# A decoder layer on one core: one projection behind each of the first score bursts, three buffers for split terms, and some work given to other engines

## The chip, the cores and the metric

The kernel runs on one core of a Trainium2 chip. The metric is the device time of one execution in microseconds (us). The time before is the median of three runs. Readers of the profile meet five engines: PE (TensorE), DVE (VectorE), ACT (ScalarE), POOL (GpSimd) and SP (SyncE, which here only issues DMAs). Each goes through its own list of instructions in order and waits on semaphores.

## What is computed

One post-norm decoder layer on 32 sequences of 128 tokens with 128 features, 16 heads of width 8, all in float32 at the interface:

```
x = layernorm(x + self_attention(x))                  # softmax over 128 keys, q/k/v with biases
x = layernorm(x + cross_attention(ctx, x, ctx))       # one 8x8 matrix per q, k, v for all heads, then Wo
x = layernorm(x + ffn(x))
# ffn: out = qlinear(gelu(qlinear(x, W1, b1)), W2, b2)
# qlinear(x, W, b): x quantised with ONE min and max over the whole tensor (affine, 8 bit),
#                   W symmetric (8 bit), integer product, times both scales, plus b
```

The minimum and maximum over the whole tensor part the program in stages: nothing of the feed-forward can start before all of attention is done, and its second product waits for all of the gelu.

## The kernel before, in words

**Tasks and slots.** A task is one batch's attention of one kind, self ("S") or cross ("C"); 64 tasks stand in the list `SEQ`, always in pairs of batches. Six self pairs come first (`LEAD_PAIRS`), then cross and self pairs in turn, then the last cross pairs. The engines are written as loops over slots k from -5 to 67 (`over_slots`). In slot k PE computes the first scores of task k+2 and the second, shifted scores of tasks k and k-1, the products with v of task k-1, transposes for k-2 and the output projection for k-3; DVE takes the maxima of task k+2 (`maximum(0)` and `maximum(1)`, L944, each over eight heads), the reciprocal and scaling of k-2, the sum of k-3, and the normalisation (`new_x`, L936) five slots behind; ACT takes the exponentials (L759, L768) and the copies out of PSUM; POOL computes 1/sqrt of the variance (L584, L587) and splits. Slot -2 holds the first maxima.

**Bursts.** `scores(0)` and `scores(1)` on PE are the two bursts of a slot. Each writes half of the heads to PSUM (`ps_s1`, banks 0 and 1) for DVE's maximum and, interleaved, half of the shifted scores (`ps_s2`, banks 2 and 3) for ACT's exponential. A burst waits for the maximum and the exponential before, and the first burst of a pair waits until its stacks have landed (`stacks_landed`).

**Projections, splits and stacks.** q and k of a pair are projected for two batches at once (L1239, L1247), evacuated by ACT (L727) and split by POOL into a float16 high and low part (`split`, L403 and L405; pair 0 by DVE) in a tile of `parts`, of which each name (sq, sk, cq, ck) has two. SP then copies three terms of the parts to the rows of a "stack" in SBUF (`fill`, L438, three DMAs for each name); a stack is the operand of the score bursts, four stacks for each name. A split waits until the stacks of the pair two before have landed. For cross attention the queries' terms (cq) come from the transposed result of self attention. V is projected by L1253 and copied by ACT (L747). All three projections write bank 7 (`ps_p`), except k of pair 0.

**The ramp.** For slots below `LEAD_SLOTS` = 2 PE issues all projections of a slot behind the second burst, later at the end of the slot (`projections(k + 1)`), q and k of a pair together. POOL makes the masked weights (`blocks`) in slot -2, and PE's three setup products (`setup_products`) follow in slot 0. `xT_in` has two tiles (`LOADS`).

**The maximum rows.** The transposed maxima are scaled by ACT and go to the stacks by a small DMA of ACT's own (L771) in each slot.

**Tail and feed-forward.** In slots 62 to 67 DVE has no maxima left; it finishes the last tasks and takes extremes of the cross results (`x2_extremes`, L916 and L917). Then the extremes go over PE (`share_extremes`), DVE works out the scales, ACT and DVE quantise x, PE transposes it and multiplies with W1, ACT applies gelu (L813), DVE takes its extremes (L1060, L1061). Ahead of the second extremes PE computes ten products that nobody reads (`unread_products`, L1375).

## Time and profile before

| | us |
| --- | --- |
| median of three runs | 337.71 |
| lowest, highest | 335.9, 339.79 |
| profiled execution | 336.97 |
| its span, first to last instruction | 335.2 |
| busy: DVE, PE, ACT, POOL | 306.8, 268.9, 248.1, 196.8 |

The rows below come from one profiled execution; times are from the start of its span. In a timeline row stand the start, the length, the engine with its line, the operation, output and input; a bracket gives the idle time before it and what ended that. "SPq" and "ACTq" are issues of DMAs by SP and ACT. A row with "x2" is two instructions in a row. In a windows row stand the stretch, its length, then busy time and number of instructions for PE, PE's weight loads (PEld), DVE, ACT and POOL, then PE's granted clock as a share of full speed, the DMA engines' share and GB/s.

### The profile page before, as it was taken

To read this page: it belongs to the slowest core of one execution; us is meant where nothing else is said; L and a number is where in the kernel's file an instruction comes from. 1 tells how busy PE (TensorE), PEld (TensorE's weight loads), DVE (VectorE), ACT (ScalarE), POOL (GpSimd) and SP (SyncE) were. 2 spreads that over 40 slices of the span, in tenths; PEclk is the share of its full clock that TensorE was granted. 3 is DMA by queue.
4 is the path that set the end of the run, shared out by engine and by line. 5 is a ranking of instruction groups with operands and counts; after the bars stand their busy time and mean duration, and the time that the engine had idled before them with its cause. 6 is when DMAs were issued, how large, how long until landed. Compare 5 with 4: busy or idle time off the path is not lost.

```text
span 335.2 us, 12397 instructions
## 1 busy us (share of the span) xinstructions
PE 268.9 (80%) x4917; PEld 168.2 (50%) x4917; DVE 306.8 (92%) x705; ACT 248.1 (74%) x502; POOL 196.8 (59%) x397
## 2 busy tenths in 40 slices
PE   4678989799999999999999988798885267416981
PEld 3355656566666666566566655555553123102551
DVE  5668899899999999999999999889989779998995
ACT  2246889688988889888888887768773299910995
POOL 2856788887667676666666846855322113901395
PEclk9999999999999999999999999989998575757896
DMA  2452424244242342424423232321100000000026
GB/s 64 115 151 85 115 77 127 59 129 116 73 122 69 113 125 64 128 59 116 118 63 114 83 113 81 107 73 52 30 3 0 1 2 0 0 0 0 2 63 189
DMA packets 48992, 25.13 MB, mean 75 GB/s; under 512 B 6440, under 2 KB 48808, under 8 KB 48936
## 3 DMA queue, kind: packets, MB, share of 16 engines
q1 hardware_dynamic: 46504, 23.74, 24.5%
q8 instruction: 39, 0.64, 0.8%
q10 hardware_dynamic: 2432, 0.60, 0.8%
q14 instruction: 17, 0.14, 0.1%
HBM read 9.39 MB, written 2.10 MB: 34 GB/s over the span
## 4 chain that ended last, share of the span: by engine, by line
DVE 41%; POOL 24%; issue 19%; PE 6%; SPq 4%; DMA 3%; ACT 2%; POOLq 1%; DVEq 0%; ACTq 0%
DVE neg_max L944 15%; DVE h_ext L1060 5%; DVE h_ext L1061 5%; POOL rstd L587 5%; SPq L438 3%; DVE arena_q L1087 2%; POOL arena_h L615 2%; POOL var_eps L584 2%; DVE arena_q L936 2%; POOL parts_ck L405 2%; PE ps L1188 2%; POOL parts_cq L405 2%; DVE o_stats L1096 2%; POOL parts_cq L403 2%; POOL parts_ck L403 2%
## 5 line engine op out<-in xcount | busy, mean ns | idle before, releaser
L944 DVE TENSOR_REDUCE neg_max<-ps 128x8 f32<-128x1024 f32 x128 | 157.1, 1227 | 10.4 <-PE ps L1188 10.0
L768 ACT ACTIVATE probs<-ps 128x1024 f32<-128x1024 f32 x64 | 65.5, 1024 | 22.8 <-PE ps L1195 22.8
L759 ACT ACTIVATE probs<-ps 128x1024 f32<-128x1024 f32 x64 | 65.6, 1024 | 16.3 <-PE ps L1195 12.8
L1188 PE MATMUL ps<-arena_h 31*128 31x128 f16 x1024 | 52.4, 220 | 21.1 <-DVE neg_max L944 11.2
L1188 PEld LDWEIGHTS ps<-arena_h 31*128 31x128 f16 x1024 | 30.6, 94 | 55.6 <-DVE neg_max L944 38.3
L1195 PE MATMUL ps<-arena_h 32*128 32x128 f16 x1024 | 51.3, 217 | 0.6 <-ACT probs L768 0.6
L584 POOL TENSOR_TENSOR var_eps<-mean_var,eps_col 128x1 f32<-128x1 f32 x64 | 12.3, 192 | 65.8 <-DVE mean_var L928 65.8
L1216 PE MATMUL ps<-probs,arena_h 128*32 128x128 f32 x1024 | 42.3, 282 | 0.2 <-issue 0.2
L1216 PE MATMUL ps<-probs,arena_q 128*32 128x128 f32 x1024 | 41.2, 279 | 0.0
L587 POOL TENSOR_TENSOR rstd<-var_eps,minus_half 128x1 f32<-128x1 f32 x64 | 35.3, 551 | 5.2 <-POOL var_eps L584 0.3
L1195 PEld LDWEIGHTS ps<-arena_h 32*128 32x128 f16 x1024 | 29.3, 93 | 1.5 <-ACT probs L768 1.0
L1216 PEld LDWEIGHTS ps<-probs,arena_h 128*32 128x32 f32 x1024 | 24.6, 110 | 7.3 <-issue 0.6
L1216 PEld LDWEIGHTS ps<-probs,arena_q 128*32 128x32 f32 x1024 | 24.0, 109 | 6.7
L1305 PE MATMUL ps<-ident,u_sb 128*128 128x128 f32 x128 | 24.7, 275 | 0.0
L1320 PE MATMUL ps<-ident,att 128*128 128x128 f32 x64 | 21.2, 331 | 4.1 <-DVE att L963 4.1
L778 ACT COPY u_sb<-ps 128x256 f32<-128x256 f32 x64 | 23.4, 366 | 0.8 <-PE ps L1216 0.8
L1060 DVE TENSOR_REDUCE h_ext<-arena_h 128x1 f32<-128x1024 f32 (+1 forms) x17 | 19.5, 1147 | 2.8 <-ACT arena_h L813 2.8
L785 ACT COPY attT<-ps 128x128 f32<-128x128 f32 x64 | 18.0, 282 | 4.9 <-PE ps L1320 4.9
L1061 DVE TENSOR_REDUCE h_ext<-arena_h 128x1 f32<-128x1024 f32 (+1 forms) x17 | 19.5, 1146 | 0.0
L954 DVE RECIPROCAL r_sum<-ps 128x16 f32<-128x16 f32 x64 | 16.6, 259 | 2.5 <-PE ps L1305 2.5
L813 ACT ACTIVATE arena_h<-ps,b_sb,quant 128x1024 f32<-128x1024 f32 (+1 forms) x17 | 18.5, 1199 | 0.3 <-PE ps L1365 0.3
L1365 PE MATMUL ps<-xqT,w_q 128*128 128x512 bf16 x32 | 14.0, 577 | 5.2 <-ACT xqT L809 4.8
(168 smaller groups left out, 618.0 us busy)
## 6 DMA issues: line engine op xcount, KB each, us to landing
arena_h<-parts_sq SPq DMA_DIRECT2D x48, 64.0 KB, 1.9
arena_h<-parts_ck SPq DMA_DIRECT2D x48, 64.0 KB, 2.3
arena_h<-parts_cq SPq DMA_DIRECT2D x48, 64.0 KB, 2.1
arena_h<-parts_sk SPq DMA_DIRECT2D x46, 64.0 KB, 2.0
xT_in<-in_xT_dram SPq DMA_DIRECT2D x16, 128.0 KB, 2.4
xN_in<-in_xN_dram SPq DMA_DIRECT2D x16, 128.0 KB, 2.3
cT_in<-in_cT_dram SPq DMA_DIRECT2D x16, 128.0 KB, 2.5
cN_in<-in_cN_dram SPq DMA_DIRECT2D x16, 128.0 KB, 2.4
```

The costliest lines, as they stand in the source:

```text
L587: pool.tensor_tensor(rstd[v.place][:, :], var_eps[v.par][:, :], minus_half[:, :], ALU.pow).then_inc(rq, 1)
L759: act.activation(probs[1][:, :], ps_s2, ACT.Exp, scale=SCALE).then_inc(ex, 1)
L768: act.activation(probs[0][:, :], ps_s2, ACT.Exp, scale=SCALE).then_inc(ex, 1)
L778: act.copy(u_sb[:, :], ps_u[:, 0:2 * S]).then_inc(ue, 1)
L944: dve.tensor_reduce(neg_max[b.par][:, HH * half:HH * half + HH], ps_s1.rearrange("p (h k) -> p h k", h=HH), AXX, ALU.max, negate=True).the ...
L1060: dve.tensor_reduce(h_ext[:, 0, col:col + 1], h, AXX, ALU.max).then_inc(f_mx, 1)
L1061: dve.tensor_reduce(h_ext[:, 1, col:col + 1], h, AXX, ALU.min, negate=True).then_inc(f_mx, 1)
L1188: ins = pe.matmul(ps_s1[:, at:at + S], q[r:r + MAX_AT, j, :], kk[r:r + MAX_AT, j, :], start=True, stop=True, skip_group_check=True)
L1195: ins = pe.matmul(ps_s2[:, at:at + S], kk[r:r + GROUP_ROWS, j, :], q[r:r + GROUP_ROWS, j, :], start=True, stop=True, skip_group_check=True)
L1216: last = pe.matmul(ps_u[32 * j:32 * j + 32, half * S:(half + 1) * S], heads_of[:, HQ * (GROUPS_HALF * half + g) + j, :], probs[half][:, (H ...
L1305: last = pe.transpose(ps_t[:, blk * S:(blk + 1) * S], u_sb[:, blk * S:(blk + 1) * S], ident[:, :])
L1320: pe.transpose(ps_x[:, 0:S], att[:, :, :].rearrange("p h e -> p (h e)"), ident[:, :]).then_inc(ta, 1)
```

## The change

1. `parts` has three tiles for each name (`PARTS`), and a split waits for the stacks of the pair three before. A cross queries' split also may come one slot sooner for two late pairs (`cq_pairs`).
2. The three DMAs of the first cross pair's queries (cq, pair 0) are issued by ACT in slot 8, behind its DMA of maximum rows, after a wait for the split, instead of by SP.
3. In slots -2 to 2 the projections stand singly behind the bursts as the table `RAMP` says: v of pair 1 behind the first burst of slot -2, q of pair 2 behind the second, and so on. k of pairs 1 and 2 is written to `ps_u`, v of pairs 1 and 2 to banks 2 and 3; ACT evacuates each of them singly. The setup products come behind the second burst of slot 0; POOL makes the masked weights there too and splits pair 3 earlier.
4. `xT_in` has four tiles (`X_LOADS`); pairs 2 and 3 are loaded at the start.
5. The normalised rows of the tasks at positions 58 to 61 are made by POOL (a negated mean, then one tensor_scalar) instead of by DVE.
6. Six unread products stand ahead of the first `share_extremes`, four behind it.

```diff
-LOADS = 2
+PARTS = 3
+LOADS, X_LOADS = 2, 4
-LEAD_SLOTS = 2
+RAMP = {(-2, 0): ("v", 1), (-2, 1): ("q", 2), (-1, 0): ("k", 2), (-1, 1): ("v", 2), (0, 0): ("q", 3),
+        (1, 0): ("k", 3), (1, 1): ("v", 3), (2, 0): ("q", 4), (2, 1): ("k", 4)}
+RAMP_FIRST, RAMP_LAST = -2, 2
+def by_pool(t):
+    return TASKS - 6 <= t.pos < TASKS - 2
...
-    free = [C_POS[2 * (i - 2)] - FILL_AT + 1 if i > 1 else FIRST_SLOT for i in range(PAIRS)]
+    free = [C_POS[2 * (i - RING)] + 2 if i >= RING else FIRST_SLOT for i in range(PAIRS)]
...
         def k_sums(i):
-            return ps_u[:, 0:PAIR] if i == 0 else ps_p[:, PAIR:2 * PAIR]
+            return ps_u[:, 0:PAIR] if i < 3 else ps_p[:, PAIR:2 * PAIR]
+        def v_sums(i):
+            return bank(1 + i)[:, 0:2 * D] if i in (1, 2) else ps_p[:, 0:2 * D]
...
-            hi, lo = parts[name][i % 2][:, 0, :], parts[name][i % 2][:, 1, :]
-            if i > 1:
-                eng.wait_ge(*stacks_landed(name, i - 2))
+            hi, lo = parts[name][i % PARTS][:, 0, :], parts[name][i % PARTS][:, 1, :]
+            if i >= PARTS:
+                eng.wait_ge(*stacks_landed(name, i - PARTS))
...
@@ SP @@
             sp.dma_start(wv_sb[:, :], wv).then_inc(w_v, 16)
+            load_xT(2)
+            load_xT(3)
...
                 for i in cq_pairs(k):
-                    ring_free(C_POS, i)
-                    fill("cq", Q_PARTS, i)
+                    if i > 0:
+                        ring_free(C_POS, i)
+                        fill("cq", Q_PARTS, i)
@@ POOL, slot(k) @@
+                    if by_pool(v):
+                        done = made_to(v.pos, True)
+                        need(pool, xc, done - 2)
+                        pool.tensor_tensor(minus_mean[v.par][:, :], mean_var[v.place][:, 0:1], minus_col[:, :], ALU.mult).then_inc(nm, 1)
...
-                i = S_FIRST.get(k + QK_AT)
-                if i:
+                i = 3 if k == 0 else S_FIRST.get(k + QK_AT)
+                if i and not (i == 3 and k != 0):
+                    if i == 3:
+                        blocks()
...
-                    blocks()
+                if k == 1:
+                    pool.wait_ge(eqk, 2 * 3 + 2)
+                    split(pool, "sk", k_full[:, :], 3)
+                for v in crosses:
+                    pool.wait_ge(rq, v.pos + 1)
+                    pool.tensor_scalar(x2_all[:, v.m, :], y_sb[v.place][:, :], minus_mean[v.par][:, :], rstd[v.place][:, :],
+                                       ALU.add, ALU.mult).then_inc(xc, 1)
@@ ACT, slot(k), in order: exponential, maximum rows, then @@
-                if k >= LEAD_SLOTS:
+                if RAMP_FIRST < k <= RAMP_LAST:
+                    ramp_out(k, 0)
+                elif k == RAMP_LAST + 1:
+                    ramp_out(RAMP_LAST, 1)
+                elif k > RAMP_LAST:
                     evacuations()
...
+                if 0 in cq_pairs(k):
+                    act.wait_ge(c_cleared, 1)
+                    act.wait_ge(split_done["cq"], 1)
+                    for t, part in enumerate(Q_PARTS):
+                        act.dma_start(stack["cq"][0][t::ROW_STEP, :, :],
+                                      parts["cq"][0][:, part, :]).then_inc(stacks_landed("cq", 0)[0], 16)
-                if k < LEAD_SLOTS:
+                if k < RAMP_FIRST:
                     evacuations()
+                elif k == RAMP_FIRST:
+                    ramp_out(k, 0)
+                if k < RAMP_LAST:
+                    ramp_out(k, 1)
@@ PE, slot(k) @@
+                def ramp(half):
+                    name, i = RAMP.get((k, half), (None, None))
+                    if name == "q":
+                        if i < 4:
+                            pe.wait_ge(eqk, 2 * i - 1)
+                        else:
+                            pe.wait_ge(evv, i)
+                        project_q(i)
+                    if name == "k":
+                        pe.wait_ge(eqk, 2 * i if i < 3 else 2 * i + 1)
+                        project_k(i)
+                    if name == "v":
+                        if i > 2:
+                            pe.wait_ge(eqk, 2 * i + 2)
+                        project_v(i)
...
-                if k == LEAD_SLOTS:
-                    projections(k)
+                ramp(0)
                 scores(1)
                 product(1)
-                if k < LEAD_SLOTS:
+                if k < RAMP_FIRST:
                     projections(k)
+                if k == 0:
+                    setup_products()
+                if k < RAMP_LAST:
+                    ramp(1)
...
+            pe.wait_ge(w_ints, 2)
+            pe.wait_ge(mx, 2 * TASKS)
+            unread_products(6)
             share_extremes(0)
-            pe.wait_ge(w_ints, 2)
+            unread_products(4)
```

## Rows read from the trace of the kernel before

**Rows 1.** Windows of two stages, the middle and the tail of attention

```profile
30.00:245.00 215.00, 198.03 (x4333) 129.50 (x4333) 208.16 (x473) 178.50 (x397) 146.17 (x299) 0.99 0.32 92
245.00:263.50 18.50, 10.14 (x159) 6.39 (x159) 17.04 (x55) 8.77 (x16) 5.17 (x14) 0.84 0.01 1
```

**Rows 2.** All instructions of line 944: durations in ns, first and last start

```profile
L944 DVE TENSOR_REDUCE neg_max<-ps x128: 1184/1225/1643, 12.7 to 243.9; 128x8 f32<-128x1024 f32 x128
```

**Rows 3.** Timeline of DVE in the ramp

```profile
18.45 1.22 DVE L944 TENSOR_REDUCE neg_max<-ps 128x8 f32<-128x1024 f32 x1 [0.71 <-PE ps L1188]
20.99 1.23 DVE L944 TENSOR_REDUCE neg_max<-ps 128x8 f32<-128x1024 f32 x1 [1.31 <-PE ps L1188]
...
29.07 1.23 DVE L944 TENSOR_REDUCE neg_max<-ps 128x8 f32<-128x1024 f32 x1 [0.47 <-PE ps L1188]
...
33.58 1.22 DVE L944 TENSOR_REDUCE neg_max<-ps 128x8 f32<-128x1024 f32 x1 [0.97 <-PE ps L1188]
```

**Rows 4.** Timeline of PE: projections of q (L1239) and k (L1247)

```profile
18.33 1.22 PE L1239 MATMUL ps<-xT_in,wq_g 128*128 128x256 f32 x2
...
26.64 0.70 PE L1239 MATMUL ps<-xT_in,wq_g 128*128 128x256 f32 x2
27.18 0.59 PE L1247 MATMUL ps<-xT_in,wk_g 128*128 128x256 f32 x2
```

**Rows 5.** Timeline of ACT and its DMA issues, early and in slot 8

```profile
8.06 1.35 ACTq L736 DMA_DIRECT2D arena_h<-parts_sk  x2
9.51 0.43 ACT L747 COPY arena_q<-ps 128x128 f32<-128x128 f32 x2 [2.00 <-DVE arena_h L881]
...
17.12 1.11 ACTq L771 DMA_DIRECT2D arena_h<-max_rows  x1
...
54.63 0.37 ACT L778 COPY u_sb<-ps 128x256 f32<-128x256 f32 x1
```

**Rows 6.** Timelines of POOL, SP and DVE around slot 10

```profile
53.92 0.67 POOL L405 TENSOR_TENSOR parts_cq<-cq_full,parts_cq 128x256 f16<-128x256 f32 x1
...
55.44 1.90 SPq L438 DMA_DIRECT2D arena_h<-parts_cq  x3
...
60.77 1.22 DVE L944 TENSOR_REDUCE neg_max<-ps 128x8 f32<-128x1024 f32 x1 [1.52 <-PE ps L1188]
```

**Rows 7.** The chain that ended last, before slot 10: start, us, what

```profile
56.74 3.54 DMA arena_h<-parts_cq
```

**Rows 8.** Timelines of POOL and DVE late in attention

```profile
207.93 0.61 POOL L403 TENSOR_TENSOR parts_cq<-cq_full,zero_col 128x256 f16<-128x256 f32 x1 [1.99 <-DMA arena_h<-parts_ck]
...
212.83 0.35 DVE L936 TENSOR_SCALAR arena_q<-y_sb,mean_var,rstd 128x128 f32<-128x128 f32 x1 [1.08 <-POOL rstd L587]
...
218.83 0.26 DVE L954 RECIPROCAL r_sum<-ps 128x16 f32<-128x16 f32 x1 [0.96 <-PE ps L1305]
```

**Rows 9.** Windows: two gaps of the middle, and after the unread products

```profile
59.00:60.00 1.00, 0.00 (x0) 0.00 (x0) 0.25 (x2) 0.00 (x0) 0.85 (x3) 1.00 0.04 4
...
217.00:218.00 1.00, 1.00 (x15) 0.62 (x8) 0.87 (x1) 0.73 (x2) 1.00 (x2) 0.50 0.33 98
...
306.00:308.00 2.00, 0.27 (x1) 0.08 (x1) 1.57 (x4) 0.00 (x0) 0.00 (x0) 1.00 0.00 0
```

**Rows 10.** Timelines of DVE and POOL in the tail of attention

```profile
250.59 0.51 DVE L936 TENSOR_SCALAR x_all<-y_sb,mean_var,rstd 128x128 f32<-128x128 f32 x2
...
255.75 0.19 POOL L584 TENSOR_TENSOR var_eps<-mean_var,eps_col 128x1 f32<-128x1 f32 x1 [2.81 <-DVE mean_var L928]
```

**Rows 11.** Timeline: DVE behind the first gelu, PE's unread products

```profile
270.22 0.69 DVE L1060 TENSOR_REDUCE h_ext<-arena_h 128x1 f32<-128x512 f32 x1 [2.51 <-ACT arena_h L813]
...
300.29 4.43 PE L1375 MATMUL ps<-w_q 128*128 128x512 bf16 x10 [9.27 <-DVE h_ext L1061]
```

**Rows 12.** Timeline of DVE: two long normalisations

```profile
43.91 2.12 DVE L936 TENSOR_SCALAR arena_q<-y_sb,mean_var,rstd 128x128 f32<-128x128 f32 x1
...
200.86 0.70 DVE L936 TENSOR_SCALAR x_all<-y_sb,mean_var,rstd 128x128 f32<-128x128 f32 x1
```

More of the change, by code:

```diff
@@ L139, in outputs, with made_to @@
     return [task(p) for p in places if task(p) is not None]
+def by_pool(t):
+    return TASKS - 6 <= t.pos < TASKS - 2
+def made_to(p, pool):
+    return sum(by_pool(t) == pool for t in SEQ[:max(p + 1, 0)])
 def tasks_to(k):
@@ L224, in decoder_layer @@
         arena_q = sb("arena_q", [128, NHC * B * S // 2])
-        xT_in = [sb(f"xT_in{i}", [128, PAIR]) for i in range(LOADS)]
+        xT_in = [sb(f"xT_in{i}", [128, PAIR]) for i in range(X_LOADS)]
         cT_in = [sb(f"cT_in{i}", [128, PAIR]) for i in range(LOADS)]
@@ L262, in decoder_layer @@
         rstd = [sb(f"rstd{i}", [128, 1]) for i in range(4)]
+        minus_mean = [sb(f"minus_mean{i}", [128, 1]) for i in range(2)]
         x2_all = sb("x2_all", [128, B, D])
@@ new lines, in k_out, with v_out @@
+                def k_out(i):
+                    act.wait_ge(pqk, 2 * i + 2)
+                    need(act, split_done["sk"], i)
+                    act.activation(k_full[:, :], k_sums(i), ACT.Identity, bias=bqk_sb[:, 1:2]).then_inc(eqk, 1)
+                def v_out(i):
+                    if i == 0:
+                        act.wait_ge(cleared, 1)
+                        act.wait_ge(split_hi["sk"], 1)
+                        for t in (0, 2):
+                            act.dma_start(stack["sk"][0][t::ROW_STEP, :, :],
+                                          parts["sk"][0][:, K_PARTS[t], :]).then_inc(stacks_landed("sk", 0)[0], 16)
+                        act.wait_ge(v0_ready, 2)
+                    elif i == 1:
+                        act.wait_ge(v_ready, 1)
+                    act.wait_ge(pvv, i + 1)
+                    if i >= RING:
+                        act.wait_ge(pv, 2 * S_POS[2 * (i - RING) + 1] + 2)
+                    src = v_sums(i).rearrange("p (b i j e) -> p b i j e", b=4, i=2, j=4)
+                    for col in range(2):
+                        last = act.copy(v_places(v_pair("S", i % RING), col, 16 * col, E), src[:, :, col, :, :])
+                    last.then_inc(evv, 1)
@@ L741, in evacuations @@
[L741 to L748 removed]
+                        v_out(i)
@@ L1353, in share_extremes, with unread_products @@
                           skip_group_check=True).then_inc(f_all, 1)
+            def unread_products(count):
+                for _ in range(count):
+                    pe.matmul(bank(0), w1_q[:, 0:128], w2_q[:, :], start=True, stop=True)
+            pe.wait_ge(w_ints, 2)
+            pe.wait_ge(mx, 2 * TASKS)
+            unread_products(6)
             share_extremes(0)
-            pe.wait_ge(w_ints, 2)
+            unread_products(4)
             turn_x(0)
@@ L1370, in _ @@
                     turn_x(c + 2)
-            def unread_products(count):
-                for _ in range(count):
-                    pe.matmul(bank(0), w1_q[:, 0:128], w2_q[:, :], start=True, stop=True)
             pe.wait_ge(f_g, NU + 1)
```

123 lines of the change are left out of this document (67 added, 56 removed).

## The prediction

> **What bounds the kernel now.** I read the windows by stage first. In the 215 us from 30 to 245 VectorE (DVE) is busy 208.2, TensorE (PE) 198.0, ScalarE (ACT) 178.5, GpSimd (POOL) 146.2; in the tail of attention, 245 to 263.5, DVE is busy 17.0 of 18.5 and the others about half [rows 1]. So the middle and the tail get shorter only where DVE idles or does less. Its pace is that of the 128 maxima (L944), two for each slot, from 12.7 to 243.9: 3.6 us a slot in the mean [rows 2]. Down DVE's timeline the reader should look at the brackets: idle time stands before single maxima of the ramp (slots 0, 2 and 3) [rows 3], before slot 10 (1.52) [rows 6], and twice late, 1.08 and 0.96 [rows 8]. Everywhere else DVE has at most short gaps. Last I read what ended each of these waits.
>
> **The ramp.** PE issues a burst of scores only after whatever stands ahead of it. The maximum at 20.99 (slot 0) waited 1.31 us where its neighbour waited 0.71, because the projections of pair 2 stood before the burst: 0.60 goes. The one at 29.07 (slot 2) waited 0.47 for the split terms of pair 2. In the change q and k of that pair are projected a half slot or more earlier, and their splits and DMAs follow: 0.47 goes, and no more, since DVE works up to the gap. The one at 33.58 (slot 3) waited 0.97 behind q and k of pair 4. There only k stays, and q takes the place of v in slot 2 at a like price; q's part, start of q to start of k, is 0.54 [rows 4]: that goes. The smaller waits in slots 4 and 5 stay, for their projections aren't touched. Sum 1.61 us [rows 3, 4].
>
> Three things are added. (1) k of pair 2 stands behind the first burst and the transpose of slot -1, which end near 16.8; the projection takes about 1.2, and the next burst could start at 17.8: +0.2. (2) ACT evacuates k of pair 2 before it issues the DMA of the maximum rows, which went at 17.12 [rows 5] and now goes near 18.5, while its reader, the second burst of slot 0, is wanted near 21 instead of 22.2. I charge 0.3. (3) In the ramp PE runs at about half speed by its durations (q 1.22 at 18.33, 0.70 at 26.64) [rows 4]. The projections now fill the holes between the early bursts, and I expect PE at its full pace before slot 0; three bursts of 0.6 us lose a quarter or more: -0.5. The other moves cost nothing while they are covered: v of pair 1 lies under a maximum of 1.2 us; the setup products wait for POOL's masks, which now come behind the split of k of pair 2 and are ready near 22, when PE has just issued the second burst of slot 0. Without cover each would cost its own length, 0.6 to 1.2. The two extra loads of x are issued by SP in a time in which it has nothing to do. The ramp is worth -1.6, bounds -0.5 (each new projection sticks out a little) and -2.4 (full pace from slot -1 on).
>
> **First cross queries by ACT.** Slot 10 waited for the last DMA of the cross queries' terms. POOL had finished the split at 54.6 (53.92 and 0.67), SP began to issue at 55.44, and the last DMA was 3.54 us under way [rows 6, 7]. The change gives these three to ACT, which goes through its instructions in order. It must wait for the split, and an issue takes it 0.6 to 0.7 (1.35 for two at 8.06; the copy behind them starts only at 9.51) [rows 5]. So ACT is free near 56.5. Queued behind stand the copy of u (at 54.63 before [rows 5]), two more copies and the exponential of slot 9. u's copy leads over PE's transposes to DVE's reciprocal; the exponential frees the bank that the next burst writes. All of it is 1.9 us late, and DVE's second maximum of slot 9 with it, less some 0.2 of slack: +1.7. Slot 10's 1.52 goes, since terms issued until 56.5 land by 60.0 even with 3.54, and slot 10 doesn't ask for them before 60.8. Net +0.2. Bounds: -1.5 (the issues lie under the exponential before) and +0.9 (the loss in full, and a landing 0.5 late).
>
> The Trainium skill, DMA: Bandwidth & Descriptors, section "Issuing engines are not separate DMA queues", speaks against this part: DMAs of all engines run on the same 16 DMA engines, so another issuer saves only issuing time. The trace agrees as far as it goes: SP began 0.8 us after the split was done, and the larger part was the transfer's own 3.54 us [rows 6, 7]. By the rule no more than those 0.8 us is to be had, which leads to the same sum.
>
> **Ring of three.** A split waits until the stacks of two pairs earlier have landed. Late in attention this shows on the cross queries' split, the longer time for 1.99 us before 207.93. It made POOL so late that rstd came only at 212.8, and DVE idled 1.08 [rows 8]. With three buffers the split waits for a pair landed some 7 us before, so POOL's 2 us go and DVE's 1.08 with them; POOL idles 0.5 to 2.7 us in most slots around, so nothing is late next. After the stall PE's granted clock is at the lower level, 0.50 in 217 to 218, where it is 1.00 elsewhere in the middle, and there falls the wait of 0.96 for PE's transposes [rows 8, 9]. I take it for a consequence of the gap: -1.0. It need not be one: between 59 and 60 PE did nothing at all, and the clock stayed at 1.00 [rows 9]. Together -2.1, bounds 0 and -2.5.
>
> **Tail.** POOL makes the normalised rows of four tasks in place of DVE. On DVE two of them take 0.51 together and the two others 0.26 each (the pair is in [rows 10]); by the starts of the instructions behind them 0.42, 0.17 and 0.17. DVE has no gap there, and the steps of PE and ACT follow from DVE's: -0.76. POOL idles 2.8 us a slot [rows 10]. It adds for each task a negated mean and the rows themselves, for which the nearest row is the split's second step, 0.67 for twice the width [rows 6]: 0.6 in all. The readers, DVE's extremes, come a slot or more later. Bounds -0.3 and -0.8.
>
> **Ahead of the feed-forward.** Ten unread products keep PE at work, six in its idle time before the extremes, four under DVE's scale arithmetic. Ten of them took 4.43 us before the second extremes, so six end about 0.6 before the first are ready. Those ten brought the clock from 0.50 to 1.00 [rows 9, 11]. If six and four do so too before the first transposes of x, the chain to the first gelu, in which DVE waits 2.51 us [rows 11], loses a part of its PE time: -0.4, bounds 0 and -0.9. Behind it DVE sets the pace, and a faster PE is worth nothing.
>
> **Sum.** -1.6 + 0.2 - 2.1 - 0.8 - 0.4 = -4.7 us on the profiled execution's 336.97 (span 335.2 and 1.8 around it): 332.3. That execution lies 0.7 under the median 337.71; I forecast 332.5. One per cent, 3.4 us, is about what a measurement of this kernel tells from no change, for its three runs span 3.9.
>
> **The rivals.** *The issues hide.* POOL's split ends a little earlier and ACT's issues lie under the exponential; slot 9 loses about 0.4 and slot 10's 1.52 is gained: 331.2. Against it: POOL works from 46 to 54.6 without a pause, so its load fixes the place of the split, and the change leaves that load. Chance 0.13.
>
> *The late gain isn't kept.* The clock falls anyway, or the new hole of 1.9 us in slot 9 brings a fall of its own, or another late arrival takes the stall's place: 2.1 shrinks to 0, which gives 334.6. For it: the clock fell behind a gap once and once not. Chance 0.21.
>
> *It doesn't do what it says.* PE's new order holds bursts in the ramp as long as the old one did, so 1.6 shrinks to 0.1, and ACT's issues cost 0.9 net instead of 0.2; the ring, the tail and the feed-forward remain: 334.7, and with half the ring's gain 335.7. Chance 0.08.
>
> *Slower: DVE and POOL collide.* DVE's normalisation (L936) takes 0.34 as a rule. It took 2.12 at 43.91 under POOL's memsets and 0.70 at 200.86 under a split, 0.36 more than the rule [rows 12]. From 72 to 187 there is nothing of the kind, since POOL's long steps fall beside it. The shorter ramp and the hole in slot 9 shift POOL against DVE. If the new phase collides in every slot of 64 to 187, some 34, that costs 12 us: 344.7; in every second, 338.6. The point is 13 collisions, where the 4.7 are eaten. Against it: POOL waits for DVE's mean and variance in each slot, which pulls the phase back. Chance 0.08. The Trainium skill, GPSIMD Engine Reference, section "Key points", has the rule behind it: GpSimd shares its SBUF interfaces with VectorE and contends with its two-port modes. The trace agrees [rows 12].
>
> **How the numbers follow.** Forecast 0.50 (331 to 334), the rivals as above. The range 329.5 to 337.0 takes in the hidden issues with the fast ramp at its low end and the two weaker cases at its high end; it leaves out the collisions and the far ends of the rest. Faster by over 1% (below 334.3): 0.49 of the forecast, 0.13, and 0.02 of the late rival, 0.64. Slower by over 1%: 0.06. Within: 0.30.
>
> **What would show it.** DVE's first maximum of slot 2 near 27.9 and of slot 3 near 32; no idle time before slot 10, but 1.5 to 2 us before the reciprocal and second maximum of slot 9, with ACT silent behind three issues; no wait of POOL for landed terms; granted clock 1.00 from 30 to 245; four L936 fewer on DVE; the first gelu 0.4 sooner after the extremes. I am wrong if new waits stand in slots -2 to 1, if the clock falls in the middle, or if L936 often takes over 0.4.

## The result

The changed kernel took 335.05 us in the median of 20 runs (333.5 to 336.34), the kernel before 336.53 in 20 runs on the same chip (335.15 to 341.7). The ratio is 0.9934, with a 95% interval of 0.9914 to 0.9955. That is a gain of 0.66%, some 2.2 us; the two medians by themselves differ by 1.5 us, 0.44%. The forecast was 4.7 us on the profiled execution. The time lies inside the range given, 329.5 to 337.0, but that says little: the kernel before, with 336.53 over 20 runs, lies inside it too, for the forecast had started from 337.71, the median of three. The class that came true is "within 1%", which had a chance of 0.30 against 0.64 for a gain of over 1%. The ratio here and below is the one on record; it can differ from the quotient of the two medians by up to 0.003. The profiled execution of the changed kernel took 335.09 us, with a span of 333.4 against 335.2 before.

In the windows of the two attention stages the reader sees nothing of note beside [rows 1]: DVE is as busy in the middle as it was, and the tail has lost 0.3 of DVE. The columns are those of [rows 1].

```profile
30.00:245.00 215.00, 199.16 (x4360) 130.09 (x4361) 208.68 (x477) 179.45 (x397) 144.12 (x297) 0.99 0.32 90
245.00:263.50 18.50, 12.41 (x141) 6.81 (x138) 16.75 (x52) 7.24 (x12) 6.75 (x20) 0.77 0.01 2
```

Stage sums don't tell where 1.8 us went. Points in time do: the first maximum (L1024 now) of each slot marks where a slot begins. The table is worked out from these starts in DVE's timelines of both kernels.

| stretch | before | after | change | forecast |
| --- | --- | --- | --- | --- |
| start to slot 9 | 55.41 | 55.00 | -0.41 | -1.6 |
| slots 9 to 11 | 12.53 | 13.54 | +1.01 | +0.2 |
| slots 12 to 32 | 73.38 | 73.90 | +0.52 | 0 |
| slots 33 to 49 | 60.26 | 59.54 | -0.72 | 0 |
| slots 50 to 54 | 19.69 | 17.59 | -2.10 | -2.1 |
| slots 55 to 60 | 20.86 | 20.86 | 0 | 0 |
| slot 61 to the extremes' last step | 21.18 | 20.80 | -0.38 | -0.76 |
| from there to the first extremes of gelu | 6.91 | 6.84 | -0.07 | -0.4 |
| from there to the end of the span | 65.0 | 65.3 | +0.3 | 0 |

The two middle rows are hiccups. Before, slot 33 took 4.04 us where its neighbours take 3.46 to 3.50, and in the changed kernel it doesn't (in one other of the fourteen profiles it does, 4.03); slots 12 to 16 lost 0.5, most of it by short waits. One normalisation took 2.15 us there, at 68.10, under POOL's memsets; before, the like stood at 67.29 with 2.08.

**The ramp.** DVE's timeline of the changed kernel, to be held against [rows 3]. The waits of 1.31 and 0.97 are down to 0.79 and 0.37 and the one of 0.47 at slot 2 is gone, but the second maximum of slot 0 (22.40) and both of slot 1 (24.52 and 26.96) wait longer: 0.72, 0.90 and 0.62, where before it was 0.51, 0.50 and nothing.

```profile
20.46 1.22 DVE L1024 TENSOR_REDUCE neg_max<-ps 128x8 f32<-128x1024 f32 x1 [0.79 <-PE ps L1273]
22.40 1.23 DVE L1024 TENSOR_REDUCE neg_max<-ps 128x8 f32<-128x1024 f32 x1 [0.72 <-PE ps L1273]
24.52 1.22 DVE L1024 TENSOR_REDUCE neg_max<-ps 128x8 f32<-128x1024 f32 x1 [0.90 <-PE ps L1273]
26.96 1.22 DVE L1024 TENSOR_REDUCE neg_max<-ps 128x8 f32<-128x1024 f32 x1 [0.62 <-PE ps L1273]
29.29 1.21 DVE L1024 TENSOR_REDUCE neg_max<-ps 128x8 f32<-128x1024 f32 x1
...
33.18 1.23 DVE L1024 TENSOR_REDUCE neg_max<-ps 128x8 f32<-128x1024 f32 x1 [0.37 <-PE ps L1273]
```

PE's timeline goes with that. A projection of 128x256 twice takes 1.06 to 1.22 at half pace and 0.60 to 0.70 at full pace. Before, the two halves of one stood at 0.70 and 0.59 from 26.64 on [rows 4], and a value projection took 0.71 at 22.61 already. Now the one at 25.60 still took 0.98, and the first at full pace stands at 27.42:

```profile
20.53 1.06 PE L1314 MATMUL ps<-xT_in,wq_g 128*128 128x256 f32 x2
25.60 0.98 PE L1321 MATMUL ps<-xT_in,wk_g 128*128 128x256 f32 x2
27.42 0.71 PE L1328 MATMUL ps<-wv_sb,xT_in 128*128 128x128 f32 x4
```

**Slot 9.** ACT's timeline shows three DMA issues, 1.89 us, and everything queued behind them; DVE's shows who waited (the first fence is ACT's, the second DVE's). The wait of 1.52 before slot 10 [rows 6] is down to 0.63, and one of 2.29 has come before the reciprocal.

```profile
54.27 1.89 ACTq L842 DMA_DIRECT2D arena_h<-parts_cq  x3
56.20 0.37 ACT L853 COPY u_sb<-ps 128x256 f32<-128x256 f32 x1 [1.86 <-issue]
```

```profile
58.52 0.26 DVE L1034 RECIPROCAL r_sum<-ps 128x16 f32<-128x16 f32 x1 [2.29 <-PE ps L1416]
...
61.47 1.23 DVE L1024 TENSOR_REDUCE neg_max<-ps 128x8 f32<-128x1024 f32 x1 [0.63 <-PE ps L1273]
```

The terms themselves came in good time: the last of the three DMAs was issued at 55.5 and landed within 2.2 us. PE stood 1.66 us for the copy of u, and behind that its granted clock (column after POOL's) was at the lower level:

```profile
57.00:58.00 1.00, 1.00 (x16) 0.76 (x5) 0.00 (x0) 1.00 (x3) 0.92 (x3) 0.54 0.07 19
58.00:60.00 2.00, 2.00 (x36) 1.06 (x34) 1.48 (x4) 1.19 (x2) 1.27 (x2) 0.50 0.04 14
```

**Late in attention.** The 1.99 of POOL for landed terms and the 1.08 and 0.96 of DVE [rows 8] are gone. The cross queries' split that had waited now comes a slot sooner, at 202.84, and no split waits; the clock is 1.00 throughout. (POOL's timeline, then a window.)

```profile
202.84 0.61 POOL L426 TENSOR_TENSOR parts_cq<-cq_full,zero_col 128x256 f16<-128x256 f32 x1
203.53 0.67 POOL L428 TENSOR_TENSOR parts_cq<-cq_full,parts_cq 128x256 f16<-128x256 f32 x1
...
207.74 0.61 POOL L426 TENSOR_TENSOR parts_ck<-ck_full,zero_col 128x256 f16<-128x256 f32 x1
208.43 0.67 POOL L428 TENSOR_TENSOR parts_ck<-ck_full,parts_ck 128x256 f16<-128x256 f32 x1
```

```profile
200.00:245.00 45.00, 39.28 (x916) 25.24 (x906) 43.98 (x103) 36.00 (x74) 23.98 (x54) 1.00 0.24 68
```

**Ahead of the first gelu.** PE's timeline: six and four unread products. They fill a part of PE's idle time, but the clock was 0.50 from 266 to 268 all the same, when the first layer's products ran; DVE waited 2.44 where it had been 2.51 [rows 11].

```profile
257.94 2.77 PE L1475 MATMUL ps<-w_q 128*128 128x512 bf16 x6
261.46 0.37 PE L1467 MATMUL ps<-ident,ext 128*2 128x128 f32 x1 [0.75 <-DVE ext L1128]
262.46 0.58 PE L1469 MATMUL ps<-top_diag,ones 2*128 2x2 f32 x2 [0.62 <-DVE top_diag L1099]
262.97 1.89 PE L1475 MATMUL ps<-w_q 128*128 128x512 bf16 x4
265.27 1.03 PE L1461 MATMUL ps<-ident_b,x_int 128*128 128x128 bf16 x8 [0.41 <-DVE x_int L1137]
266.56 1.95 PE L1490 MATMUL ps<-xqT,w_q 128*128 128x512 bf16 x4 [0.25 <-ACT xqT L884]
```

### The profile page after: what moved, and what is told of

It reads as the page before. It is cut to its first block, busy times and chain, and to the rows that moved or that the text cites. A ratio compares the mean times of both kernels' runs of the same rounds, so it can differ in the third digit from the quotient of the medians.

```text
span 333.4 us, 12425 instructions
## 1 busy us (share of the span) xinstructions
PE 275.9 (83%) x4927; PEld 170.3 (51%) x4927; DVE 305.9 (92%) x701; ACT 248.7 (75%) x502; POOL 198.8 (60%) x405
## 3 DMA queue, kind: packets, MB, share of 16 engines
q1 hardware_dynamic: 46072, 23.55, 24.4%
## 4 chain that ended last, share of the span: by engine, by line
POOL 40%; issue 24%; DVE 23%; PE 9%; ACT 2%; POOLq 1%; ACTq 1%; DVEq 0%
POOL rstd L619 7%; DVE h_ext L1142 5%; DVE neg_max L1024 5%; DVE h_ext L1143 5%; POOL var_eps L612 3%; POOL arena_h L649 3%; POOL parts_cq L428 3%; POOL parts_ck L428 3%; POOL parts_cq L426 3%; POOL parts_ck L426 3%; POOL x_bias L638 2%; PE ps L1273 2%; POOL o_root L747 2%; POOL parts_sk L428 2%; POOL parts_sq L428 2%
## 5 line engine op out<-in xcount | busy, mean ns | idle before, releaser
L1024 DVE TENSOR_REDUCE neg_max<-ps 128x8 f32<-128x1024 f32 x128 | 157.4, 1230 | 9.2 <-PE ps L1273 9.2
L820 ACT ACTIVATE probs<-ps 128x1024 f32<-128x1024 f32 x64 | 65.6, 1025 | 14.3 <-PE ps L1280 10.9
L1304 PE MATMUL ps<-probs,arena_q 128*32 128x128 f32 x1024 | 42.2, 283 | 1.9 <-ACT u_sb L853 1.9
L1304 PE MATMUL ps<-probs,arena_h 128*32 128x128 f32 x1024 | 41.3, 279 | 0.0
L1475 PE MATMUL ps<-w_q 128*128 128x512 bf16 x28 | 12.7, 629 | 9.0 <-DVE h_ext L1143 9.0
```

Of the source, the lines that this page charges most:

```text
L820: act.activation(probs[1][:, :], ps_s2, ACT.Exp, scale=SCALE).then_inc(ex, 1)
L1024: dve.tensor_reduce(neg_max[b.par][:, HH * half:HH * half + HH], ps_s1.rearrange("p (h k) -> p h k", h=HH), AXX, ALU.max, negate=True).the ...
L1304: last = pe.matmul(ps_u[32 * j:32 * j + 32, half * S:(half + 1) * S], heads_of[:, HQ * (GROUPS_HALF * half + g) + j, :], probs[half][:, (H ...
```

## The experiments

Twelve runs in three groups of four; the kernels of a group ran on one chip beside the kernel before (medians 338.66, 336.58 and 337.5), so absolute times are compared within a group and the ratio across groups. The changed kernel itself stands in none of the three. The first group takes the change apart.

**ring_only.** The kernel before with the ring of three alone.

```diff
+PARTS = 3
-    free = [C_POS[2 * (i - 2)] - FILL_AT + 1 if i > 1 else FIRST_SLOT for i in range(PAIRS)]
+    free = [C_POS[2 * (i - RING)] + 2 if i >= RING else FIRST_SLOT for i in range(PAIRS)]
... [i % 2] -> [i % PARTS], stacks_landed(name, i - 2) -> (name, i - PARTS)
```

> The kernel before with three buffers for split terms and nothing else. Theory: POOL's waits for landed terms (1.4 and 2.0 us) and DVE's 1.08 us go, and the clock fall behind them with 0.96 more, so the time is 2.0 us (0.6%) under before. Rival: the late clock fall comes by itself and moves elsewhere; then 1.1 us or less.

335.68 us (6 runs), ratio 0.9885, 0.9851 to 0.992. Slots 50 to 54 took 17.59 us as in the changed kernel, and the clock was 1.00 from 200 to 245. It also had no wait before slot 10, though SP issued the terms: slots 9 to 11 took 10.68. But it had reached slot 9 1.3 us later, mostly by waits of PE for landing key terms: 1.37 at the end of slot 1, where it had been 0.85, and one in slot 5 that hadn't been there (PE's timeline):

```profile
45.50 0.23 PE L1189 MATMUL ps<-arena_h 31*128 31x128 f16 x1 [1.19 <-DMA arena_h<-parts_sk]
```

So the edit is worth 2.1 us there. It has two parts, the third buffer and the cross queries' split one slot sooner, and no run takes one without the other. The ring alone has no worse a ratio than the whole change, whose interval reaches from 0.9914 to 0.9955; the two weren't timed on one chip.

**ramp_only.** The ramp and the two x tiles alone: two parts buffers, SP's transfers, no rows by POOL, no products ahead of the extremes.

```diff
-PARTS = 3
+PARTS = 2
-    return TASKS - 6 <= t.pos < TASKS - 2
+    return False
-            unread_products(6)
-            unread_products(4)
... and cq_pairs and SP's transfers as in the kernel before
```

> The ramp and the four tiles for x alone, with two buffers, cross queries by SP, DVE making all rows, no products before the first extremes. Theory: slot 3 starts 0.4 us earlier than before as in the changed kernel, because TensorE reaches its full pace at 26 us instead of 22; the total is within 0.3% of before and the late stall is there again. Rival: the late full pace was chance, then slot 3 starts 1.2 us earlier or more.

337.78 us (12 runs), ratio 0.9984, 0.9951 to 1.0018: no change that can be told. Slot 3 came 0.41 sooner than before, as in the changed kernel. Slots 50 to 54 took 19.87, with POOL's wait in the same place. So the ramp was worth 0.4 in both profiles and not 1.6, and the late stall belongs to the ring of two. (POOL's timeline.)

```profile
209.97 0.61 POOL L426 TENSOR_TENSOR parts_cq<-cq_full,zero_col 128x256 f16<-128x256 f32 x1 [3.09 <-DMA arena_h<-parts_ck]
```

**cq_by_sp.** The changed kernel with the first cross queries' DMAs back on SP.

```diff
-                    if i > 0:
-                        ring_free(C_POS, i)
-                        fill("cq", Q_PARTS, i)
+                    ring_free(C_POS, i)
+                    fill("cq", Q_PARTS, i)
@@ ACT @@
-                if 0 in cq_pairs(k): ... three act.dma_start
```

> The changed kernel with the first cross queries' DMAs back on SP. Theory: ACT's three issues (1.9 us) made everything behind them late, DVE lost 2.3 us before the reciprocal of slot 9, and the hole brought TensorE's clock down to 0.50 for 3 us. Then slots 9 and 10 together take 8.8 us as before instead of 10.1, the clock stays at 1.00 there, and the time is 1.0 to 1.5 us under the changed kernel (some 0.989 of before). Rival: the wait before slot 10 comes back in full (1.5 us) and brings the clock fall with it, since the hole is the same; then no difference from the changed kernel.

335.65 us (7 runs), ratio 0.9894, 0.9855 to 0.9932. The wait before slot 10 was back (1.31 on DVE, 1.63 on PE), the one before the reciprocal gone, slots 9 to 11 took 12.10 against 13.54, and the clock stayed at 1.00 through the hole. In the profiles the 1.4 us are as expected; the ratio can't be told from the changed kernel's, since the intervals overlap. It is the same as that of the ring alone on the same chip, 335.65 against 335.68 us.

```profile
58.00:59.00 1.00, 0.00 (x0) 0.00 (x0) 0.64 (x2) 0.20 (x2) 0.91 (x2) 1.00 0.04 4
59.00:60.00 1.00, 0.49 (x24) 0.39 (x28) 0.04 (x1) 0.01 (x1) 0.92 (x4) 1.00 0.20 60
```

**cq_by_sp_fill.** The same with two unread products in PE's idle time at 6.9 and 8.6 us, to bring PE to its full pace ahead of the bursts. Theory: half pace is what eats the ramp's gain. The products' results are read by nobody.

```diff
+                    if i == 0:   # behind k of pair 0
+                        pe.matmul(bank(0)[:, 0:S], wq_g[:, :], xT_in[0][:, 0:S], start=True, stop=True, ...)
+                    if i == 0:   # behind v of pair 0
+                        pe.matmul(bank(0)[:, 0:PAIR], wq_g[:, :], xT_in[0][:, :], start=True, stop=True, ...)
```

> As cq_by_sp, and two float32 products that nobody reads fill TensorE's idle time from 6.9 to 7.5 and 8.8 to 9.9 us. Theory: what TensorE did before decides when it runs at full pace; busy without a gap from 3.7 us it has it by 20 us, q's projection of pair 3 takes 0.7 instead of 1.06, and slot 3 starts 0.8 us or more earlier than in cq_by_sp. Rival: the early float32 work doesn't bring it sooner, and slot 3 starts where it does in cq_by_sp, within 0.1 us.

332.55 us (6 runs), ratio 0.9801, 0.9763 to 0.9838, and slot 3 at 32.56 against 32.99. I took the theory for shown at this point, though two of its own signs had failed: slot 3 came 0.43 sooner and not 0.8, and q of pair 3 still took 1.06, at 20.16. The third group took the gain back.

The second group builds on this kernel, but has no run of it, so a run there is held against the profile of cq_by_sp_fill and not against its time.

**loads_later.** SP's loads of slot 7 issued in slot 8, behind the cross fill.

```diff
-                for i in xT_pairs(k):
-                    load_xT(i)
...
+                for m in {7: (), 8: (7, 8)}.get(k, (k,)):
+                    for i in xT_pairs(m):
+                        load_xT(i)
```

> Base: the changed kernel with the first cross queries' transfers back on SP and two unread products early in the ramp (0.9801 of the kernel before). Alone changed: SP's loads of slot 7 are issued in slot 8, behind the first cross fill, so three issues of some 0.63 us leave the queue ahead of the fill. Theory (the wait of about 1.3 us before slot 10's scores is the landing of the cross queries' terms, issued late by SP): the wait shrinks to under 0.4 us, slot 61 begins 0.9 to 1.3 us sooner than in the base, ratio about 0.977. Rival (the landing itself is slow, 1.9 to 3.3 us, whenever it starts, or the rows' own chain is as late): the wait stays at 1 us or more, ratio as the base.

331.75 us (4 runs), ratio 0.9877, 0.9835 to 0.9919. The wait before slot 10 was gone (slot 9 took 3.76 against 4.77), and a new one of 1.01 stood in slot 11 on the key terms (PE's timeline):

```profile
64.92 0.22 PE L1266 MATMUL ps<-arena_h 31*128 31x128 f16 x1 [1.01 <-DMA arena_h<-parts_sk]
```

Slots 9 to 11 took 11.70 against 11.94 in the base. Most of the wait was moved and not removed. (ffn_fill, with the loads in their old place, has one of 0.55 at the same point, so the loads aren't shown to be its cause.) Slot 61 began 1.27 us sooner than in the base, as the theory had it, but 0.72 of that was there at slot 3 already, ahead of the edit; the ratio expected, 0.977, didn't come.

**ffn_fill.** Seven, one and five unread products in place of six and four, the one between the transpose of the extremes and their product.

```diff
+                if i == 0:
+                    unread_products(1)
-            unread_products(6)
+            unread_products(7)
-            unread_products(4)
+            unread_products(5)
```

> Base as in the run before. Alone changed: the unread products around the feed-forward layer's extremes are 7, 1 and 5 in place of 6 and 4, one of them between the transposes of the extremes. Theory (TensorE comes to the first layer at half pace because it had idled behind the extremes): with the holes closed the granted clock is above 0.50 before the first gelu, and from the extremes to the first gelu 0.3 to 0.5 us less pass. Rival (what rows on VectorE take sets that stretch): the same within 0.1 us.

331.86 us (4 runs), ratio 0.9876, 0.9836 to 0.9916. From the extremes' last step to the first extremes of gelu it took 6.11 us; the nine profiles with six and four products took 6.53 to 6.85 (table below). The clock was 1.00 from 260 to 264, where the first layer runs, and its transposes took 0.82 instead of 1.03 (windows and PE's timeline):

```profile
260.00:264.00 4.00, 2.57 (x17) 0.95 (x14) 1.80 (x10) 3.32 (x6) 0.00 (x0) 1.00 0.01 2
```

```profile
258.13 0.38 PE L1475 MATMUL ps<-w_q 128*128 128x512 bf16 x1
258.91 0.38 PE L1469 MATMUL ps<-top_diag,ones 2*128 2x2 f32 x2 [0.41 <-DVE top_diag L1091]
259.22 1.25 PE L1475 MATMUL ps<-w_q 128*128 128x512 bf16 x5
261.52 0.82 PE L1459 MATMUL ps<-ident_b,x_int 128*128 128x128 bf16 x8 [1.05 <-DVE x_int L1129]
```

In this run there was no wait before slot 10 either, with SP's loads in their old place. So loads_later alone doesn't show that the loads' place ended that wait. What the runs without it share is how early SP began to issue the cross queries' three transfers: 0.47 to 1.08 us before slot 9 began, in ffn_fill, loads_later, all_pieces and ring_only. In the eight with the wait it began 0.09 before to 0.54 after. In these eight the split had been done for 0.7 us or more; SP was still issuing the three transfers of the cross keys (2.77 us of issues in the kernel before).

**ramp_fill2.** One more unread product behind q and behind k of pair 2.

```diff
+                    if i == 2:      # in project_q and in project_k
+                        pe.matmul(bank(5)[:, 0:S], wq_g[:, :], xT_in[1][:, 0:S], start=True, stop=True, ...)
```

> Base as before. Alone changed: one more unread 128-column product behind the third query projection and behind the third key projection, in a bank that nobody reads then. Theory (in the base TensorE lost its full pace at about 18 us because the projections had been spread over its idle time): the full pace holds through 18 to 24 us, slot 3 begins 0.3 to 0.8 us sooner than in the base, and that stays to the end. Rival (the pace falls whatever is put there, and the two products delay the bursts): slot 3 begins 0 to 0.5 us later.

333.78 us (10 runs), ratio 0.9904, 0.987 to 0.9938. Slot 3 at 32.50 against 32.56 in the base and 31.84 and 31.86 in the two runs before. PE kept its full pace to 20 us, and the granted clock was 0.50 from 20 to 26. In this one profile more products moved the low stretch and didn't remove it: the theory failed.

**rows_by_dve.** The normalised rows of the last tasks by DVE again; a single execution. (The expectation calls them maximum rows; those stayed as they were.)

```diff
-    return TASKS - 6 <= t.pos < TASKS - 2
+    return False
```

> Base as before. Alone changed: the maximum rows of the last tasks are again written by VectorE and not by GpSimd. Prediction's own price of the move: 0.76 us, so the first extremes of the feed-forward layer come 0.76 us later than in the base, counted from slot 61's first maximum. Theory now (the row write had covered the reciprocal's own wait): 0.3 to 0.45 us later.

From slot 61 to the extremes' last step 21.17 us against 20.80: 0.37, as the later theory said. DVE's timeline shows the reason. With the row write (L1008 here) the reciprocal, the write and `att` begin 0.17 apart:

```profile
254.35 0.25 DVE L1026 RECIPROCAL r_sum<-ps 128x16 f32<-128x16 f32 x1
254.52 0.26 DVE L1008 TENSOR_SCALAR x_all<-y_sb,mean_var,rstd 128x128 f32<-128x128 f32 x1
254.69 0.28 DVE L1035 TENSOR_TENSOR att<-ps,r_sum 128x128 f32<-128x128 f32 x1
```

and without it, in the changed kernel, `att`, which reads the reciprocal's result, begins 0.28 behind it. Of 0.34 between the two starts only 0.06 goes.

```profile
252.31 0.25 DVE L1034 RECIPROCAL r_sum<-ps 128x16 f32<-128x16 f32 x1
252.59 0.29 DVE L1043 TENSOR_TENSOR att<-ps,r_sum 128x128 f32<-128x128 f32 x1
```

This run had also the base's instructions up to slot 55, and its ramp was 0.5 slower (slot 3 at 33.05). That made me doubt the first group's reading, and so the third group asks what the early products and ACT's issues are worth, side by side.

**no_fill_again** and **fill_again.** cq_by_sp and cq_by_sp_fill, unchanged.

> The changed kernel with the first cross queries' transfers back on SP, once more, to stand beside the same kernel with the two early unread products on the same chip. Theory (the unread products bring TensorE to its full pace sooner in most executions): this one is 1 to 3 us slower than the next. Rival (in which microsecond the pace rises varies from execution to execution, products or not, as four profiles with equal instructions up to 24 us differed by up to 0.9 us at slot 3): the two differ by under 0.5 us.

> The same kernel plus the two early unread products. Theory: 1 to 3 us faster than the run before, ratio to the kernel before 0.982 to 0.986. Rival: within 0.5 us of the run before.

334.15 us (8 runs), ratio 0.9903, 0.987 to 0.9936, and 334.19 us (11 runs), 0.9908, 0.9878 to 0.9938: no difference. The gain of 3 us in the first group didn't come again. (The expectation speaks of up to 0.9 us at slot 3; cq_by_sp_fill, loads_later, ffn_fill and rows_by_dve lay up to 1.21 apart there.) The profiles do differ, by 1.07 at slot 3. In fill_again the pace rose at 10 us, fell at 16.7 and was back near 26 (PE's timeline):

```profile
10.00 0.70 PE L1306 MATMUL ps<-xT_in,wq_g 128*128 128x256 f32 x2 [0.35 <-ACT arena_q L792]
...
15.06 0.60 PE L1313 MATMUL ps<-xT_in,wk_g 128*128 128x256 f32 x2
16.70 1.22 PE L1323 MATMUL ps<-wv_sb,xT_in 128*128 128x128 f32 x4
...
24.44 1.06 PE L1313 MATMUL ps<-xT_in,wk_g 128*128 128x256 f32 x2
26.93 0.71 PE L1323 MATMUL ps<-wv_sb,xT_in 128*128 128x128 f32 x4
```

**change_fill.** The whole change as it was, ACT's issues included, with the two early products.

> The whole change as it was, the first cross queries' transfers issued by ACT, plus the two early unread products. Theory (ACT's three issues of 0.63 us delay the copy of u and leave a hole of 1.7 to 2.3 us before slot 10's reciprocal, at times with a fall of the clock): 1 to 2 us slower than the run with SP's issues, and DVE waits over 2 us near slot 9. Rival (the holes even out by the end): within 0.5 us of it.

333.9 us (7 runs), ratio 0.9895, 0.9857 to 0.9934: as SP's version beside it, where 1 to 2 us more had been expected. In the profile ACT's three issues cost again: 1.72 before the reciprocal, slots 9 to 11 12.61 against 12.14 in fill_again. The clock this time stayed at 1.00. (DVE's timeline.)

```profile
57.33 0.26 DVE L1034 RECIPROCAL r_sum<-ps 128x16 f32<-128x16 f32 x1 [1.72 <-PE ps L1422]
```

**all_pieces.** SP's transfers, early products, later loads, and seven, one and five products.

> Transfers on SP, early unread products, SP's loads of slot 7 behind the cross fill, unread products 7, 1 and 5 around the feed-forward extremes. Theory: 0.3 to 1.2 us faster than with the early products alone, ratio 0.979 to 0.984, no wait over 0.5 us before slot 10. Rival (what is won at the feed-forward layer or before slot 10 is lost to the run's own spread): within 0.3 us of the run with the early products alone.

332.09 us (6 runs), ratio 0.9845, 0.9809 to 0.9881, 2.1 us under fill_again, more than the 0.3 to 1.2 expected. No wait before slot 10 (slots 9 to 11: 11.15), and 6.20 from the extremes to gelu's; in the profiles these two make 1.3 of it. It is 1.5% under the kernel before, where the change, on another chip, gives 0.7%.

The stretches of all profiles, worked out as in the first table ("rise": start of the first projection that took its short length, 0.59 to 0.71, by PE's timeline):

| kernel | rise | slot 3 | slots 9 to 11 | slots 50 to 54 | slot 61 to extremes | to gelu's |
| --- | --- | --- | --- | --- | --- | --- |
| before | 22.6 | 33.58 | 12.53 | 19.69 | 21.18 | 6.91 |
| after | 27.4 | 33.18 | 13.54 | 17.59 | 20.80 | 6.84 |
| ring_only | 22.6 | 34.09 | 10.68 | 17.59 | 21.18 | 6.91 |
| ramp_only | 27.4 | 33.17 | 13.85 | 19.87 | 21.17 | 6.93 |
| cq_by_sp | 25.5 | 32.99 | 12.10 | 17.59 | 20.80 | 6.84 |
| cq_by_sp_fill | 14.3 | 32.56 | 11.94 | 17.59 | 20.80 | 6.85 |
| loads_later | 11.0 | 31.84 | 11.70 | 17.59 | 20.80 | 6.54 |
| ffn_fill | 11.0 | 31.86 | 11.23 | 17.58 | 20.80 | 6.11 |
| ramp_fill2 | 10.0 | 32.50 | 13.70 | 17.59 | 20.79 | 6.63 |
| rows_by_dve | 27.3 | 33.05 | 12.09 | 17.59 | 21.17 | 6.84 |
| no_fill_again | 27.6 | 33.68 | 13.79 | 17.58 | 20.78 | 6.54 |
| fill_again | 10.0 | 32.61 | 12.14 | 17.59 | 20.80 | 6.53 |
| change_fill | 14.2 | 32.58 | 12.61 | 17.58 | 20.78 | 6.54 |
| all_pieces | 10.0 | 32.65 | 11.15 | 17.58 | 20.79 | 6.20 |

The reader should see two kinds of columns. Slots 50 to 54 (the ring) and slot 61 to the extremes (the rows) are the same to 0.02 wherever the edit is the same. Those of the ramp and of slots 9 to 11 move by over a microsecond among kernels with equal instructions there. The last column is of both kinds: seven, one and five products give 6.11 and 6.20 and no products 6.91 to 6.93, but six and four give 6.84 or 6.85 in four profiles and 6.53 to 6.63 in five.

## Why the prediction was right or wrong

**The ring, right.** -2.1 forecast, -2.10 measured, in 12 of 12 profiles with three buffers and in neither of the two with two (19.69 and 19.87). Nothing took the stall's place there, and the clock stayed up, so the rival in which the late gain shrinks to 0 is out. One condition of that rival did come: the new hole in slot 9 brought a fall of the clock of its own, from 57 until past 60. It was paid in slots 9 to 11 and not late. "If the clock falls in the middle" was also one of the two signs of being wrong that came; the other was new waits in slots -2 to 1.

The rival that came closest is the one with the chance of 0.08, that the change doesn't do what it says: it had the ramp at 0.1, ACT's issues at +0.9 and 334.7 to 335.7, and the time is 335.05. That the whole time fell into the range is luck in part: of five terms only one had its size, and two lay outside their own bounds. The steps:

**The ramp, the step that failed most: "I expect PE at its full pace before slot 0".** Its parts by the bursts were right in sign: slot 0 came 0.53 sooner (0.60 forecast), the wait of slot 3 fell by 0.60. The pace went the other way. Before, PE ran at full pace from the value projection at 22.61 on at the latest; with the projections spread singly it was at half pace into the one at 25.60. Slot 1 began 0.07 and slot 2 0.22 later than before, and slot 3 only 0.40 sooner: 0.4 at slot 9 instead of 1.6, outside the bound of -0.5. The charge of 0.2 for the key projection didn't come: the maximum behind it began at 18.44, before at 18.45 [rows 3]. The 0.3 for the maximum rows can't be told from the pace. Nor is it one profile's chance that the 1.6 didn't come: with the new ramp and no early products slot 3 stood at 32.99, 33.17, 33.18 and 33.68, with the old one at 33.58 and 34.09. Whether the pace alone ate the 1.2 isn't shown, nor what made it rise later. Products put early did raise it early and brought slot 3 to between 31.84 and 32.65 in seven of eight profiles, but the eighth, with the same instructions up to 14 us, had its rise at 27.3 and slot 3 at 33.05, and the one pair of kernels timed in two groups gave 3.1 us once and nothing the second time. What stays open is how much of that reaches the end in the mean of many executions.

**The first cross queries, direction right, size wrong.** The chain was as described: ACT's 1.89 us, u's copy at 56.20, the second maximum of slot 9 late. I took +1.7 for it against -1.5 for slot 10's wait. It became +2.34 (that maximum began 4.07 us after the first instead of 1.73) against -1.23 (slot 10 began 2.40 us behind it instead of 3.63, with PE at its lower clock and 0.63 still waited). Sum +1.11, of which 0.1 is back by slot 12: +1.01 instead of +0.2, just outside the bound of +0.9, and +0.5 against SP's version where no fall of the clock came (change_fill against fill_again). Against SP's version the whole time shows nothing that can be measured on one chip, 333.9 and 334.19. The premise was weak too: the wait before slot 10 isn't a fixed 1.5. With SP as issuer PE waited there for 1.25 to 2.12 us in eight profiles, before's 1.83 among them, and hardly in four. In the eight the slowest of the three transfers took 3.1 to 3.8 us to land, in the four, and whenever ACT issued, 1.9 to 2.2. What slows it isn't shown. The Trainium skill, DMA: Bandwidth & Descriptors, section "Issuing engines are not separate DMA queues", says that another issuer saves only the issuing time, which is usually small. Here the prediction drew from it that no more than 0.8 us was to be had. The terms in fact landed more than that sooner: by 57.7 at the latest in the changed kernel, at 59.5 in cq_by_sp, with slot 9 at nearly the same place (55.00 and 54.81). Nor was the issuing time small for the engine that took it over, 0.63 us for each DMA, with a critical copy behind them.

**The tail, half.** "-0.76" summed the removed instructions' own time. 0.38 went, since all four rows had stood between a reciprocal and its reader, two of them behind the same one: the distance of the two fell from 0.59, 0.33 and 0.34 to 0.28 each. The bounds, -0.3 to -0.8, held it.

**Ahead of the feed-forward, nearly nothing in this profile, up to the forecast in others.** -0.07 for -0.4. "If six and four do so too" was the step: in the changed kernel's profile the clock was at 0.50 from the first of the ten products to the layer. With the same six and four it had risen to 1.00 by the transpose of the extremes in four profiles, where four products took 1.04 instead of 1.89, and it was back at 0.50 when the layer began; these four took 6.53 or 6.54, which is the forecast -0.4. PE's timeline of fill_again, its clock 1.00 from 260 to 262 and 0.50 from 264 to 266:

```profile
260.97 1.04 PE L1473 MATMUL ps<-w_q 128*128 128x512 bf16 x4
263.27 1.03 PE L1459 MATMUL ps<-ident_b,x_int 128*128 128x128 bf16 x8 [1.26 <-DVE x_int L1129]
264.55 1.95 PE L1488 MATMUL ps<-xqT,w_q 128*128 128x512 bf16 x4 [0.25 <-ACT xqT L876]
```

In a fifth the clock rose only with the layer itself (6.63). So the mechanism was right in part, and whether it acts varies. With seven, one and five the clock was 1.00 at the layer in both profiles, after an idle time of 1.05: 6.11 and 6.20 against 6.91 before.

**Collisions of DVE and POOL, no.** Beside the ones of 2.12 at 43.51 and 2.15 at 68.10, which the kernel before has as well (2.12 and 2.08), there was no row of them; slots 17 to 60 took 3.45 to 3.5 each but for a few. The rival with them is out. Another part of what was missing, some 0.15, is the sum of the middle and the last stretch, hiccups that no part of the change explains.

Together: 1.2 (ramp), 0.8 (ACT), 0.4 (tail), 0.3 (feed-forward) and 0.15 make, but for rounding, the 2.9 us by which the profile's -1.8 missed -4.7.

## What to carry to other kernels

Time an edit by pairs on one chip and more than once before believing a gain that rests on TensorE's pace or on a transfer's landing: one comparison gave 3 us here, its repetition nothing, while gains that rest on a wait removed for good (the ring of three) or on instructions taken away came out the same to 0.02 us in every profile. Count DMA issues given to a compute engine as time of that engine, if critical work is queued behind them: here they cost 0.5 to 1.4 us of slots 9 to 11 against SP's version, though the whole time showed no difference that could be measured. And price a removed instruction by the start of the one behind it that has to wait for something else: if it stood between a result and its reader, it was partly free.

## What the runs showed of the hardware

**TensorE's pace early in an execution varies with equal instructions.** Eight profiles have the two early products and equal instructions on PE up to 14 us; two kernels were profiled twice. The first projection at full pace stood at 10.0 (three), 11.0 (two), 14.2 to 14.3 (two) and 27.3 (one). The same kernel had it at 14.3 and 10.0 (cq_by_sp_fill, fill_again), another at 25.5 and 27.6 (cq_by_sp, no_fill_again). Which it was went with over 1 us at slot 3. The best was the middle one: after a rise at 11.0 PE was at half pace again from 19.3, and slot 3 came at 31.84 and 31.86; after one at 10.0 it was so from 16.7 in two profiles and from 20 in ramp_fill2, in all three until after 24.4, and slot 3 came at 32.50 to 32.65. The Trainium skill, TensorE: Matmul & The Clock Gate, section "What's actually happening", says that the same kernel shows a different number of slow products from run to run; these runs agree, with the numbers above.

**The record of the granted clock isn't to be trusted at the start.** The windows give 1.00 from 10 to 14 us in every profile, and from 20 to 24 in the changed kernel's, while projections took 1.06 to 1.22 there wherever the rise came later, some 1.75 times their later length. The durations are the thing to read.

**A hole in PE's work isn't always followed by a lower clock.** Idle times of 1.92, 1.99 and 2.12 us before slot 10 were followed by 0.50 in all three cases (slot 10 then took 4.60 to 4.77 us, elsewhere 3.41 to 3.90); 1.25, 1.29, 1.41, 1.63 and 1.83 by none; 1.66 in slot 9 once, and once not. That is the trace's list; it isn't a rule for where it turns.

**A transfer of 64 KB within SBUF doesn't always land alike.** The three of the first cross queries took 1.9 to 2.2 us each in the six profiles without a wait for them before slot 10; in the other eight the slowest took 3.1 to 3.8.
